# Attention scores of a Trainium2 megakernel: from masked f32 matmuls on 32 rows to bf16 parts on 72 rows, spread through DRAM

## The chip, the cores and the metric

One core of one Trainium2 chip runs the whole program. The metric is the device time of one execution in microseconds. The engines are PE (TensorE), DVE (VectorE), ACT (ScalarE), POOL (GpSimd) and SP (SyncE), which only issues transfers here.

## The reference, cut to what matters

The program chains four blocks over 8 sequences of 256 tokens and 128 features. The change is in the first of them, six layers of this:

```python
q = (h @ wq.T + bq_).reshape(bh, sl, H, DH)          # H = 16 heads of DH = 8
k = (h @ wk.T + bk_).reshape(bh, sl, H, DH)
scores = jnp.einsum('blhd,bmhd->bhlm', q, k) * inv_sqrt_d
w_avg = jax.nn.softmax(scores, axis=-1).mean(axis=1)
new_w = jax.nn.softmax(CSCALE * w_avg + rel[None], axis=-1)
sa = jnp.einsum('blm,bme->ble', new_w, h)
h1 = _ln(h + sa, l1w, l1b)
h2 = _ln(h1, l2w, l2b)
ff = jax.nn.relu(h2 @ w1.T + b1_) @ w2.T + b2_
return (_ln(h2 + ff, l3w, l3b), None)
```

Each head has only 8 dimensions, so a score is a sum of 8 products in f32.

## The kernel before

`stage_a` is the six layers; `stage_b`, `stage_c` and `stage_d` follow, each in a block of its own that starts when the one before has ended, and nothing in them changes. Stage A lasts from the start to about 1264 us.

The order of stage A is written out as a table of slots, `slots_a`. A sequence has 8 slots (`QSLOTS`); a slot covers 4 heads (`CH`) for one half of the 256 queries. Sequence `q` of layer `l` starts at slot `at = 64 * l + 8 * q`, and its later steps (mixing, normalizing, the hidden layer) stand at fixed slots behind that, so they fall beside the scores of the next sequences. In what follows "slot 0" to "slot 7" are slots modulo 8. Every engine walks the same table in order and skips what is not its own, so each engine's queue is strictly in table order; semaphores hold the engines together. Within a slot, `in_order` puts some kinds first and some last.

The steps of one slot: PE makes the scores of 4 heads into one of two PSUM buffers (`score`); DVE takes the negated row maximum of each half (`max0`, `max1`, L506); ACT makes the four exponentials one slot later (`exp`, L405); DVE inverts the row sums (L547) and adds two of the four heads into a PSUM sum (L483, L486, L495); POOL scales an identity matrix by the other two heads' inverse sums (`diag`, L308), with which PE adds those heads (`head_sum`, L639, last in its slot). `score` of a slot waits until the exponentials of two slots before have been read.

Steps once in a sequence that matter here, with their slots: DVE adds the hidden layer's output (L573) and takes its statistics (L521 with `a_h`) in slot 7; POOL turns them into a deviation (`rstd` part 2, L316 to L326), then applies the second gain (`affine` part 1, L352 and L355), both slot 7; DVE takes the statistics of the attended rows (L521 with `a_r`) in slot 0 and POOL turns these into a deviation (`rstd` part 0, again L316 to L326), slot 0; DVE normalizes with it (`norm` part 0, L528 with `a_r`), slot 1; POOL applies the first gain (`affine` part 0, L339 and L342, which reads `rows1`), slot 2; DVE takes the statistics of that in slot 4; `rstd` part 1 follows on POOL in slot 4. PE's last matmuls of the hidden layer (`mlp`, L673) stand in slot 7.

The scores before: `project` (slot 2) makes `qT` and `kT` in f32, `mask` on POOL (slot 3, last in the slot) writes `km`, four copies of `kT` each masked to one head of a 32-row group, and `score` runs two f32 matmuls of 32 rows and 512 columns side by side on two row groups.

SP loads the next layer's weights in a loop of its own, each group as soon as the last user of the old weights is done.

## Time and profile before

| | |
|---|---|
| median of 3 runs | 2278.96 us (2277.47 to 2282.62) |
| profiled execution, its own time | 2278.32 us |
| its span in the trace | 2276.4 us |
| busy share of the span: PE, DVE, ACT, POOL | 87%, 75%, 72%, 56% |
| granted clock of TensorE, mean | 0.955 |
| moved by DMA | 45.93 MB, mean 20 GB/s |

The shares are means over four stages, and PE's ends are modelled, so a PE that shows as busy need not be the limit. The profiled execution took 1.9 us more than its span, and 0.6 us less than the median.

### The profile page before, as it was taken

What the parts mean: (1) busy time and instruction counts of PE and PEld (TensorE: products, weight loads), DVE (VectorE), ACT (ScalarE), POOL (GpSimd) and SP (SyncE); (2) the same over time, 40 slices, a digit from 0 to 9 for tenths busy, and PEclk for the clock granted to TensorE, in tenths of its full rate; (3) what the DMA queues carried; (4) which work ended last, traced back from release to release, by engine and by line L of the source; (5) the groups of instructions that cost most, each with busy time, mean ns of one, the idle gap of its engine ahead of it and who ended that gap; (6) DMA issues with size and microseconds to landing.
All of it is one profiled execution on the core that took longest, in us unless ns stands there. A gap on an engine that the chain in (4) does not pass through costs nothing. (4 is left out here: it accounts for less than half of the span.)

```text
span 2276.4 us, 40732 instructions
## 1 busy us (share of the span) xinstructions
PE 1981.4 (87%) x9638; PEld 1254.6 (55%) x9638; DVE 1714.8 (75%) x4069; ACT 1647.2 (72%) x5239; POOL 1263.4 (56%) x2137
## 2 busy tenths in 40 slices
PE   4899999999999999999997784949995888898886
PEld 2455555555555555555555463336652666666665
DVE  5999999899899989999995425068876666766673
ACT  3888888788888878888884231459962778787874
POOL 2566766676667667667666333048874434443440
PEclk9999999999999999999998797869996999999999
DMA  1000000000000000000000311102212000000000
GB/s 44 1 1 4 7 13 4 3 17 4 5 7 13 4 3 17 4 4 7 13 1 1 130 53 48 30 19 93 101 56 72 1 1 1 1 1 1 1 1 19
DMA packets 30509, 45.93 MB, mean 20 GB/s; under 512 B 9352, under 2 KB 21904, under 8 KB 29952
## 3 DMA queue, kind: packets, MB, share of 16 engines
q1 hardware_dynamic: 29008, 40.52, 5.6%
q0 software_dynamic: 1248, 2.59, 0.3%
q8 instruction: 91, 1.49, 0.3%
q14 instruction: 162, 1.33, 0.2%
HBM read 39.34 MB, written 5.32 MB: 20 GB/s over the span
## 5 line engine op out<-in xcount | busy, mean ns | idle before, releaser
L405 ACT ACTIVATE a_prob<-a_scores,a_negmax 128x256 f32<-128x256 f32 x1536 | 706.2, 479 | 122.0 <-DVE a_negmax L506 91.7
L506 DVE TENSOR_REDUCE a_negmax<-a_scores 128x2 f32<-128x512 f32 x768 | 525.5, 685 | 53.3 <-PE a_scores L628 44.8
L628 PE MATMUL a_scores<-a_km,a_qT 32*128 32x512 f32 x1536 | 436.3, 646 | 63.2 <-ACT a_prob L405 56.2
L639 PE MATMUL a_heads<-a_prob,a_diag 128*128 128x256 f32 x1536 | 391.3, 388 | 11.0 <-POOL a_diag L308 7.5
L308 POOL TENSOR_TENSOR a_diag<-ident,a_rowinv 128x256 f32<-128x256 f32 x384 | 240.9, 632 | 157.4 <-DVE a_rowinv L547 150.3
L405 ACT ACTIVATION_READ_ACCUMULATOR a_prob<-a_scores,a_negmax 128x1 f32 x1536 | 323.2, 210 | 0.0
L639 PEld LDWEIGHTS a_heads<-a_prob,a_diag 128*128 128x128 f32 x1536 | 280.5, 193 | 62.8 <-POOL a_diag L308 25.1
L628 PEld LDWEIGHTS a_scores<-a_km,a_qT 32*128 32x128 f32 x1536 | 117.3, 184 | 196.2 <-issue 98.3
L1374 DVE TENSOR_TENSOR_SCAN c_state<-c_decay,c_psD 128x1024 f32<-128x1024 f32 x64 | 146.1, 2286 | 34.2 <-PE c_psD L1477 23.3
L1238 POOL TENSOR_TENSOR c_du<-c_state,c_c_row 128x1024 f32<-128x1024 f32 x64 | 151.3, 2366 | 33.6 <-DVE c_state L1374 24.3
L486 DVE SCALAR_TENSOR_TENSOR a_sums<-a_prob,a_rowinv,a_sums 128x256 f32<-128x256 f32 x288 | 141.1, 490 | 29.0 <-DVE a_rowinv L547 2.0
L316 POOL TENSOR_TENSOR a_f<-a_st 128x4 f32<-128x4 f32 x144 | 29.3, 203 | 201.2 <-DVE a_st L521 201.2
L495 DVE SCALAR_TENSOR_TENSOR a_sums<-a_prob,a_rowinv,a_sums 128x256 f32<-128x256 f32 x288 | 137.8, 478 | 0.0
L1818 ACT ACTIVATE d_prob<-d_psS,d_bias,d_inv 128x128 f32<-128x128 f32 (+1 forms) x256 | 121.7, 483 | 13.1 <-DVE d_bias L1952 12.3
L2041 PE MATMUL d_psQ<-d_wqkv,d_hT 128*128 128x512 f32 x192 | 105.6, 635 | 21.6 <-DVEq L1999 19.0
L1768 POOL TENSOR_TENSOR d_qk<-d_direct,d_cross 128x512 f32<-128x512 f32 x32 | 40.6, 1268 | 150.0 <-DVE d_cross L1925 150.0
L2082 PE MATMUL d_psO<-d_val,d_probT 128*128 128x64 f32 x768 | 101.1, 268 | 21.9 <-DVE d_o_n L1964 21.9
L1496 PE MATMUL c_psY<-c_du,ident 128*128 128x512 f32 x256 | 120.1, 593 | 0.0
L666 PE MATMUL a_turn<-a_h2T,a_w 128*128 128x256 f32 x384 | 110.6, 413 | 1.4 <-DVEq L564 0.7
L673 PEld LDWEIGHTS a_turn<-a_w,a_act 128*128 128x128 f32 x768 | 92.4, 197 | 35.1 <-issue 34.1
L2082 PEld LDWEIGHTS d_psO<-d_val,d_probT 128*128 128x128 f32 x768 | 95.8, 192 | 25.6 <-issue 25.6
L666 PEld LDWEIGHTS a_turn<-a_h2T,a_w 128*128 128x128 f32 x384 | 67.5, 194 | 76.4 <-issue 69.3
(286 smaller groups left out, 4282.8 us busy)
## 6 DMA issues: line engine op xcount, KB each, us to landing
c_c_row<-c_rows SPq DMA_DIRECT2D x32, 512.0 KB, 3.6
a_w<-in_a_w SPq DMA_DIRECT2D x12, 256.0 KB, 2.6
b_w<-in_b_w SPq DMA_DIRECT2D x1, 2816.0 KB, 15.2
a_rows<-in_a_rows SPq DMA_DIRECT2D x12, 128.0 KB, 2.0
b_w<-in_b_w SPq DMA_DIRECT2D x1, 1536.0 KB, 18.2
d_wqkv<-in_d_wqkv SPq DMA_DIRECT2D x2, 768.0 KB, 5.7
b_rows_in<-in_b_blank SPq DMA_DIRECT2D x1, 1518.0 KB, 8.8
b_packed<-b_rows_in SPq DMA_DIRECT2D x5, 264.0 KB, 4.2
```

The lines of the kernel that those rows point to most:

```text
L308: g.tensor_tensor(diag[part % RING][:], ident[:].unsqueeze(1).broadcast_to([P, BH, P]), rowinv[part % RING][:, 1::BH].unsqueeze(2).broadca ...
L405: ins = a.activation(prob[part % RING][:, c, :], psS[part % 2][:, c, :], ACT.Exp, bias=negmax[part % 2][:, c:c + 1], accum_out=rowsum[part ...
L486: v.scalar_tensor_tensor(psA[:, t, :], pr[:, 0, :], inv[:, 0:1], psA[:, t, :], ALU.mult, ALU.add).then_inc(s["acc_step"], 1)
L495: v.scalar_tensor_tensor(dst[:, t, :], prob[part % RING][:, BH, :], rowinv[part % RING][:, BH:BH + 1], psA[:, t, :], ALU.mult, ALU.add).th ...
L506: v.tensor_reduce(negmax[part % 2][:, hs], psS[part % 2][:, hs, :], AX.X, ALU.max, negate=True).then_inc(s["negmax_ready"], 1)
L628: p.matmul(psS[part % 2][:, h * BH:(h + 1) * BH, :], qT[u][rows, t * P:(t + 1) * P], km[u][rows, c:c + BH, :], start=True, stop=True)\
L639: ins = p.matmul(psH[:, t, :], diag[part % RING][:, h, :], prob[part % RING][:, h * BH + 1, :], start=(j == 0 and h == 0), stop=(j == HG - ...
L666: ins = p.matmul(dst[:, k, :], w1[:, f * P:(f + 1) * P], h2T[u][:], start=True, stop=True)
L1238: g.tensor_tensor(yc[n % 2][t], state[n % 2][t][:], c_row[n % CROWS][:], ALU.mult)\
L1374: v.tensor_tensor_scan(state[n % 2][t][:], decay[n % 2][t][:].rearrange("p q l -> p (q l)"), psD[t][:], 0.0, ALU.mult, ALU.add).then_inc(s ...
L1818: ins = a.activation(prob[t][g % 2][:, j, k0:k1], psS[n % 2][:, j, k0:k1], ACT.Exp, bias=bias[n % 2][:, j:j + 1], scale=inv[q % 2][t][:, 0 ...
L2082: ins = p.matmul(psO[:, h * DHD:(h + 1) * DHD], probT[g % 2][:, j, b, :], val[q % 2][:, b, h * DHD:(h + 1) * DHD], start=(b == 0), stop=(b ...
```

## The change

q and k are each written as a sum of three bf16 numbers (24 bits of mantissa in all). ACT rounds both to bf16 (one more ACTIVATE of 128x512 in `project`), and POOL makes the two remainders in three operations of 128x512 (`split`, in place of `mask`). SP writes the three parts to a DRAM scratch and reads them back in another layout (`spread`): 72 rows hold, for each of the 8 dimensions, the 9 pairs of a part of q with a part of k. For that the keys' 24 rows are read three times over, and each of q's three parts is read three times over. The weights' rows are sorted by dimension on the host. A head's scores are then one bf16 matmul with 72 rows and 256 columns, four to a slot, and the first half's semaphore rises after two of them.

The projection, the split and the spread of a sequence stand 10, 9 and 8 slots ahead of its first score; `project` was 6 ahead and `mask` 5. Because SP now takes part in the table, its loads of the next layer's weights stand in it too (`load`, parts 0 to 4), at slots -7, 25, 30, 34 and 40 of the last sequence of a layer.

```diff
-RG = 4
-RW = P // RG
+PARTS = 3
+KROWS = PARTS * PARTS * DH
+SPREAD = 16 + PARTS * 16 + 16
...
-                place(at - 8, "per_layer", l, q, 0)
-            place(at - 6, "project", l, q, 0)
-            place(at - 5, "mask", l, q, 0)
+                place(at - 12, "per_layer", l, q, 0)
+            place(at - 10, "project", l, q, 0)
+            place(at - 9, "split", l, q, 0)
+            place(at - 8, "spread", l, q, 0)
...
+            if q == SEQS - 1 and l + 1 < LAYERS:
+                for part, slot in enumerate((-7, 25, 30, 34, 40)):
+                    place(at + slot, "load", l, q, part)
...
-        qT = two("qT", [P, L])
-        kT = sb("kT", [P, L])
-
-        km = two("km", [P, CH, L])
-        head_mask = sb("head_mask", [P, CH])
+        qk = sb("qk", [P, 2, L])
+        rest = sb("rest", [P, 2, L])
+        one = sb("one", [P, 2])
+        parts3 = ctx.enter_context(nc.sbuf_tensor("a_parts3", [P, 2, PARTS, L], BF16))
+
+        spread = [[ctx.enter_context(nc.sbuf_tensor(f"a_spread{u}_{k}", [KROWS, HEADS, L], BF16)) for k in range(2)]
+                  for u in range(2)]
+        scratch = nc.dram_tensor("a_split", (2, PARTS, P, L), BF16, kind="Internal").ap()
+        keys = scratch[1].rearrange("a (e h) t -> (a e) (h t)", h=HEADS).unsqueeze(0)\
+            .broadcast_to([PARTS, PARTS * DH, HEADS * L])
+
+        def queries(a):
+            return scratch[0, a].rearrange("(e h) t -> e (h t)", h=HEADS).unsqueeze(0)\
+                .broadcast_to([PARTS, DH, HEADS * L])
...
-                    sp.wait_ge(s["qk_ready"], n * 2)
-                    load(l + 1, *qk)
-                    sp.wait_ge(s["n1_ready"], n)
-                    sp.wait_ge(s["h2_ready"], n)
-                    load(l + 1, *norm1)
-                    sp.wait_ge(s["act_ready"], n * FC)
-                    load(l + 1, *hidden)
-                    sp.wait_ge(s["y_ready"], n)
-                    load(l + 1, *out)
-                    sp.wait_ge(s["hT_ready"], n + SEQS)
-                    sp.wait_ge(s["h_tok_ready"], n + SEQS)
-                    load(l + 1, *norm3)
+
+                def do(kind, lay, steady, q, part):
+                    m = lay * SEQS + q
+                    u = q % 2
+                    if kind == "spread":
+                        sp.wait_ge(s["split_step"], (m + 1) * 4)
+
+                        sp.wait_ge(s["spread_in"], m * SPREAD + SPREAD)
+                        sp.dma_start(scratch.rearrange("k a p t -> p (k a) t"),
+                                     parts3[:].rearrange("p k a t -> p (k a) t")).then_inc(s["spread_in"], 16)
+                        sp.wait_ge(s["spread_in"], m * SPREAD + 16 + SPREAD)
+
+                        sp.wait_ge(s["scores_ready"], ((m - 2) * G8 + G8 + 2 * G8) * HALVES)
+                        sp.dma_start(spread[u][1][:], keys).then_inc(s["spread_in"], 16)
+                        for a in range(PARTS):
+                            sp.dma_start(spread[u][0][a * PARTS * DH:(a + 1) * PARTS * DH], queries(a))\
+                                .then_inc(s["spread_in"], 16)
+                    elif kind == "load":
+                        n = (lay + 1) * SEQS
+                        if part == 0:
+                            sp.wait_ge(s["qk_ready"], n * 2)
+                        elif part == 1:
+                            sp.wait_ge(s["n1_ready"], n)
+                            sp.wait_ge(s["h2_ready"], n)
+                        elif part == 2:
+                            sp.wait_ge(s["act_ready"], n * FC)
+                        elif part == 3:
+                            sp.wait_ge(s["y_ready"], n)
+                        else:
+                            sp.wait_ge(s["hT_ready"], n + SEQS)
+                            sp.wait_ge(s["h_tok_ready"], n + SEQS)
+                        load(lay + 1, *groups[part])
...
-                    elif kind == "mask":
-                        g.wait_ge(s["qk_ready"], m * 2 + 2)
-
-                        g.wait_ge(s["scores_ready"], ((m - 2) * G8 + G8 + 2 * G8) * HALVES)
-                        g.tensor_tensor(km[u][:], kT[:].unsqueeze(1).broadcast_to([P, CH, L]),
-                                        head_mask[:].unsqueeze(2).broadcast_to([P, CH, L]), ALU.mult)\
-                            .then_inc(s["km_ready"], 1)
+                    elif kind == "split":
+                        g.wait_ge(s["split_step"], m * 4 + 1)
+                        g.tensor_tensor(rest[:], qk[:], parts3[:, :, 0], ALU.subtract).then_inc(s["split_step"], 1)
+                        g.wait_ge(s["split_step"], m * 4 + 2)
+                        g.tensor_tensor(parts3[:, :, 1], rest[:], one[:].unsqueeze(2).broadcast_to([P, 2, L]), ALU.mult).then_inc(s["split_step"], 1)
+                        g.wait_ge(s["split_step"], m * 4 + 3)
+                        g.tensor_tensor(parts3[:, :, 2], rest[:], parts3[:, :, 1], ALU.subtract)\
+                            .then_inc(s["split_step"], 1)
...
-                run(g, do, first=("diag",), last=("mask",))
+                run(g, do, first=("diag",), last=("split",))
...
-                        a.wait_ge(s["scores_ready"], ((m - 2) * G8 + G8 + 2 * G8) * HALVES)
-                        a.activation(qT[u][:], src[:, 0, :], ACT.Identity, bias=bqs[:], scale=float(DH) ** -0.5)\
+                        a.wait_ge(s["split_step"], m * 4)
+                        a.activation(qk[:, 0, :], src[:, 0, :], ACT.Identity, bias=bqs[:], scale=float(DH) ** -0.5)\
                             .then_inc(s["qk_ready"], 1)
-
-                        a.wait_ge(s["km_ready"], m)
-                        a.activation(kT[:], src[:, 1, :], ACT.Identity, bias=qk_cols[:, 1:2])\
+                        a.activation(qk[:, 1, :], src[:, 1, :], ACT.Identity, bias=qk_cols[:, 1:2])\
                             .then_inc(s["qk_ready"], 1)
 
                         a.wait_ge(s["qk_ready"], 2 * m + 2)
                         a.sem_inc(t_free[b], 1)
+
+                        a.wait_ge(s["spread_in"], (m - 1) * SPREAD + 16 + SPREAD)
+                        a.activation(parts3[:, :, 0], qk[:], ACT.Copy).then_inc(s["split_step"], 1)
...
-                        evacuated("project")
-                        p.wait_ge(s["km_ready"], m + 1)
+                        if part == 0:
+                            p.wait_ge(s["spread_in"], (m + 1) * SPREAD + SPREAD)
 
                         p.wait_ge(s["exp_done"], (n + 1) * HALVES)
-                        for h in range(HALVES):
-                            rg = (j % 2) * HALVES + h
-                            rows = slice(rg * RW, (rg + 1) * RW)
-                            c = j // 2 * BH
-                            p.matmul(psS[part % 2][:, h * BH:(h + 1) * BH, :], qT[u][rows, t * P:(t + 1) * P],
-                                     km[u][rows, c:c + BH, :], start=True, stop=True)\
-                                .then_inc(s["scores_ready"], 1)
+                        for c in range(CH):
+                            ins = p.matmul(psS[part % 2][:, c, :], spread[u][0][:, j * CH + c, t * P:(t + 1) * P],
+                                           spread[u][1][:, j * CH + c, :], start=True, stop=True)
+                            if c % BH == BH - 1:
+                                ins.then_inc(s["scores_ready"], 1)
...
-    a["a_wq"] = np.ascontiguousarray(i["L0_attn_Wq"].transpose(0, 2, 1))
-    a["a_wk"] = np.ascontiguousarray(i["L0_attn_Wk"].transpose(0, 2, 1))
+    by_dim = lambda w: w.reshape(LAYERS, HEADS, DH, -1).transpose(0, 2, 1, 3).reshape(LAYERS, E, -1)
+    a["a_wq"] = np.ascontiguousarray(by_dim(i["L0_attn_Wq"]).transpose(0, 2, 1))
+    a["a_wk"] = np.ascontiguousarray(by_dim(i["L0_attn_Wk"]).transpose(0, 2, 1))
```

On POOL, this is the place from slot 7 to slot 2 in the last layer. `a_h` is the second normalization's result, `a_f` and `a_mv` are the statistics and the deviation, `a_diag` the scaled identity, `a_n` the first normalization's result. Before:

```order
L352 TENSOR_TENSOR a_h<-a_n,a_rows 128x256
L355 TENSOR_TENSOR a_h<-a_h,a_rows 128x256
L308 TENSOR_TENSOR a_diag<-ident,a_rowinv 128x256
L316 TENSOR_TENSOR a_f_1<-a_st_1 128x2x2
L317 TENSOR_TENSOR a_f_1<-a_st_1 128x2
L319 TENSOR_TENSOR a_f_1<-a_f_1,a_parts 128x6
L321 TENSOR_TENSOR a_mv_1<-a_f_1 128x2
L322 TENSOR_TENSOR a_mv_1<-a_f_1,a_eps 128x2
L324 TENSOR_TENSOR a_mv_1<-a_mv_1 128x2
L326 TENSOR_TENSOR a_mv_1<-a_mv_1,minus_half 128x2
L308 TENSOR_TENSOR a_diag<-ident,a_rowinv 128x256 x2
```

In the changed kernel (its line numbers are some 36 higher):

```order
L388 TENSOR_TENSOR a_h<-a_n,a_rows 128x256
L391 TENSOR_TENSOR a_h<-a_h,a_rows 128x256
L333 TENSOR_TENSOR a_rest<-a_qk,a_parts 128x512
L335 TENSOR_TENSOR a_parts<-a_rest,a_one 128x2x256
L337 TENSOR_TENSOR a_parts<-a_rest,a_parts 128x2x256
L344 TENSOR_TENSOR a_diag<-ident,a_rowinv 128x256
L352 TENSOR_TENSOR a_f_1<-a_st_1 128x2x2
L353 TENSOR_TENSOR a_f_1<-a_st_1 128x2
L355 TENSOR_TENSOR a_f_1<-a_f_1,a_parts 128x6
L357 TENSOR_TENSOR a_mv_1<-a_f_1 128x2
L358 TENSOR_TENSOR a_mv_1<-a_f_1,a_eps 128x2
L360 TENSOR_TENSOR a_mv_1<-a_mv_1 128x2
```

The three operations of `split` (`a_rest`, `a_parts`) now stand between the second gain and the next `a_diag`, ahead of the deviation that DVE's normalization in slot 1 reads. The masking stood in slot 3, behind the gains.

On SP, this is what the steady loop issues; `a_rows` are the gains of the normalizations, `a_w` the hidden layer's weights, `a_cols` and `a_b` small columns. Before, the whole loop body:

```order
L249 DMA a_wq<-in_a_wq 128x128
L249 DMA a_wk<-in_a_wk 128x128
L249 DMA a_qk_cols<-in_a_qk_cols 128x2
L249 DMA a_rows<-in_a_rows 128x256
L249 DMA a_rows<-in_a_rows 128x384
L249 DMA a_cols<-in_a_cols 128x2
L249 DMA a_w<-in_a_w 128x512
L249 DMA a_b<-in_a_b 128x4
L249 DMA a_w<-in_a_w 128x512
L249 DMA a_rows<-in_a_rows 128x256
L249 DMA a_cols<-in_a_cols 128x2
```

In the changed kernel, from the spread of a new layer's fourth sequence on (`a_split` is the DRAM scratch, `a_spread_1` the keys, `a_spread_0` the queries):

```order
L281 DMA a_split<-a_parts 128x6x256
L286 DMA a_spread_1<-a_split 72x1x4096
L288 DMA a_spread_0<-a_split 24x1x4096 x3
L263 DMA a_rows<-in_a_rows 128x256
L263 DMA a_rows<-in_a_rows 128x384
L263 DMA a_cols<-in_a_cols 128x2
L263 DMA a_w<-in_a_w 128x512
L263 DMA a_b<-in_a_b 128x4
L281 DMA a_split<-a_parts 128x6x256
L286 DMA a_spread_1<-a_split 72x1x4096
L288 DMA a_spread_0<-a_split 24x1x4096 x3
L263 DMA a_w<-in_a_w 128x512
```

Each load now stands behind the spreads of the sequences ahead of it in the table: the first gains (`a_rows`, 128x256) behind that of the fourth sequence of the new layer, the output weights (the second `a_w`) behind that of the fifth.

## Rows read from the trace of the kernel before

**Rows 1.** Windows: stretch, busy us of each engine (instructions), clock, DMA share, GB/s.

```profile
100.00:1230.00 1130.00, 1067.91 (x4896) 627.40 (x4897) 1015.11 (x2539) 935.33 (x3572) 765.88 (x1741) 0.99 0.02 7
```

**Rows 2.** Instruction groups, DVE, 100 to 1260 us: busy, mean ns, idle before and releaser.

```profile
L506 DVE TENSOR_REDUCE a_negmax<-a_scores 128x2 f32<-128x512 f32 x721 | 493.6, 685 | 36.1 <-PE a_scores L628 36.0
```

**Rows 3.** Timeline of DVE, one sequence: start us, us, instruction, idle before it.

```profile
569.49 0.41 DVE L573 TENSOR_TENSOR a_h<-a_h,a_turn 128x256 f32<-128x256 f32 x1
570.06 0.49 DVE L521 BATCH_NORM_STATS2 a_st<-a_h 128x6 f32<-128x128 f32 x2 [0.15 <-DVE a_h L573]
...
571.15 0.68 DVE L506 TENSOR_REDUCE a_negmax<-a_scores 128x2 f32<-128x512 f32 x1
...
576.88 0.89 DVE L528 TENSOR_SCALAR a_r<-a_r,a_f,a_mv 128x128 f32<-128x128 f32 x2
...
586.62 0.69 DVE L506 TENSOR_REDUCE a_negmax<-a_scores 128x2 f32<-128x512 f32 x1 [0.23 <-PE a_scores L628]
...
594.57 0.49 DVE L521 BATCH_NORM_STATS2 a_st<-a_h 128x6 f32<-128x128 f32 x2 [0.15 <-DVE a_h L573]
```

**Rows 4.** Timeline of POOL over the same sequence.

```profile
570.62 0.20 POOL L316 TENSOR_TENSOR a_f<-a_st 128x4 f32<-128x4 f32 x1 [3.31 <-DVE a_st L521]
...
573.49 0.72 POOL L355 TENSOR_TENSOR a_h<-a_h,a_rows 128x256 f32<-128x256 f32 x1
574.17 0.62 POOL L308 TENSOR_TENSOR a_diag<-ident,a_rowinv 128x256 f32<-128x256 f32 x1
574.74 0.20 POOL L316 TENSOR_TENSOR a_f<-a_st 128x4 f32<-128x4 f32 x1
...
576.14 0.71 POOL L326 TENSOR_TENSOR a_mv<-a_mv,minus_half 128x2 f32<-128x2 f32 x1
...
578.51 0.91 POOL L339 TENSOR_TENSOR a_n<-a_r,a_rows 128x256 f32<-128x256 f32 x1
579.49 0.73 POOL L342 TENSOR_TENSOR a_n<-a_n,a_rows 128x256 f32<-128x256 f32 x1
...
588.28 1.36 POOL L308 TENSOR_TENSOR a_diag<-ident,a_rowinv 128x256 f32<-128x256 f32 x2
```

**Rows 5.** Timeline of PE, same stretch.

```profile
566.32 1.13 PE L628 MATMUL a_scores<-a_km,a_qT 32*128 32x512 f32 x4
567.38 2.05 PE L673 MATMUL a_turn<-a_w,a_act 128*128 128x128 f32 x16
...
571.44 1.89 PE L639 MATMUL a_heads<-a_prob,a_diag 128*128 128x256 f32 x8
```

**Rows 6.** Instruction groups of POOL, whole run, shapes apart.

```profile
L300 POOL TENSOR_TENSOR a_km<-a_kT,a_head_mask 128x1024 f32<-128x1024 f32 x48 | 90.8, 1892 | 5.7 <-ACT a_kT L392 5.7
...
L1768 POOL TENSOR_TENSOR d_qk<-d_direct,d_cross 128x512 f32<-128x512 f32 x32 | 40.6, 1268 | 150.0 <-DVE d_cross L1925 150.0
...
L1777 POOL TENSOR_TENSOR d_qk<-d_direct,d_inv 128x512 f32<-128x512 f32 x32 | 33.4, 1042 | 5.7 <-POOL d_inv L1773 5.5 <-PE d_psT L2071 0.2
```

**Rows 7.** DMA issues by line: count, KB each, median us from issue to landing.

```profile
c_c_row<-c_rows SPq DMA_DIRECT2D x32, 512.0 KB, 3.6
...
out<-x_tok SPq DMA_DIRECT2D x1, 1024.0 KB, 5.1
...
a_wq<-in_a_wq SPq DMA_DIRECT2D x6, 64.0 KB, 1.9
```

**Rows 8.** Windows, a stretch full of transfers of stage B, columns as in Rows 1.

```profile
1283.00:1288.00 5.00, 5.00 (x12) 2.93 (x13) 2.22 (x6) 1.50 (x2) 2.47 (x3) 0.51 0.98 420
```

**Rows 9.** Page, part 3: the DMA queue of SP: packets, MB, share of 16 engines.

```profile
q1 hardware_dynamic: 29008, 40.52, 5.6%
```

**Rows 10.** Timeline, start of stage A, POOL and DVE.

```profile
29.19 1.89 POOL L300 TENSOR_TENSOR a_km<-a_kT,a_head_mask 128x1024 f32<-128x1024 f32 x1 [5.24 <-ACT a_kT L392]
...
33.32 2.48 DVE L506 TENSOR_REDUCE a_negmax<-a_scores 128x2 f32<-128x512 f32 x4 [8.37 <-issue]
```

**Rows 11.** Waits of POOL, 100 to 1230 us: us in total, times, longest.

```profile
POOL a_n L339 <- DMA a_rows<-in_a_rows: 1.0, 3, 0.4
```

More of the change, by code:

```diff
@@ L249, in load @@
                         sp.dma_start(dst[:], d[name][l]).then_inc(s[signal], 16)
-                qk = ("qk_in", (wq, "a_wq"), (wk, "a_wk"), (qk_cols, "a_qk_cols"))
-                norm1 = ("norm1_in", (rows1, "a_rows1"), (rows2, "a_rows2"))
-                hidden = ("hidden_in", (cols2, "a_cols2"), (w1, "a_w1"), (b1, "a_b1"))
-                out = ("out_in", (w2, "a_w2"))
-                norm3 = ("norm3_in", (rows3, "a_rows3"), (cols3, "a_cols3"))
-                for group in (qk, norm1, hidden, out, norm3):
-                    load(0, *group)
@@ L274, in _ @@
+                run(sp, do)
             @block.gpsimd
@@ L278, in _ @@
                 g.memset(eps[:], EPS)
+                g.memset(one[:], 1.0)
                 g.memset(minus_one[:], -1.0)
```

19 lines of the change are left out of this document (11 added, 8 removed).

## The prediction

> **What bounds the kernel now.** I read the windows first. Between 100 and 1230 us, in stage A's steady part, DVE is busy 1015 of 1130 us (90%), ACT 83%, POOL 68%; PE shows 94%, but its ends are modelled, so I ask who waits for whom [rows 1]. The groups of instructions say it for DVE: of its idle time only 36 us stood before a row maximum and ended with PE's scores [rows 2]; nearly all the rest is the gap behind its own last result. So DVE sets the pace, and PE's scores can give back at most about 36 us, 0.8 per sequence.
>
> The timelines show how near other engines are to setting it. One sequence takes 24.5 us, from DVE's statistics in slot 7 at 570.06 to the same at 594.57; I call that start T [rows 3]. At T + 0.56 POOL, idle 3.31 us for it, begins the deviation, then the second gain, at T + 4.1 the scaled identity, at T + 4.7 the next deviation, whose last operation ends at 576.85, T + 6.8 [rows 4]. DVE's normalization that reads it starts at 576.88 [rows 3]. There is no slack on this stretch: POOL works through it without a gap, and DVE arrives as it ends. POOL's 3.31 us of idle time lie ahead of it and can't be used by work queued behind. The masking, 1.89 us, stands in slot 3, where nobody waits for POOL.
>
> **The split on POOL.** The masking goes (nothing gained, no wait behind it). In its place come three operations of 128x512 between the second gain and the identity, in the middle of that stretch. With two full f32 operands POOL takes 1.27 us for this shape, with one operand repeated along a row 1.04 [rows 6]; the first and third are of the one kind, the second of the other. That is 3.58, and with a step of some 0.07 us between dependent operations, as from 579.42 to 579.49 [rows 4], 3.7 us. No row has bf16 on POOL. Bounds: three times half of the masking, 2.8, and three times 1.27 with gaps, 4.0; I take 3.7, since the shape and operands are those of the rows. DVE's normalization then comes 3.7 us late in each sequence. Queued behind POOL's split are the identity of slot 0, for which PE's head sum of slot 1 and so PE's score of slot 2 wait, but DVE stands still longer than they do. Sequences 3 to 47 have a split with such a deviation behind it: 45 x 3.7 = **+166 us**, and a sequence of 24.5 + 3.7 - 0.8 = 27.4 us, the last term being the next paragraph's.
>
> **The scores on PE.** Two f32 halves now run side by side and take 1.13 us for the four records [rows 5]; both are ready near the end. Four bf16 matmuls of 256 columns stream a quarter of the f32 columns each, and the first half is ready after two. No row has such a matmul with 72 rows; the change lies between nothing (1.13 as now) and about 0.9 us earlier for the first half. DVE's waits are short, 0.23 us in such a row [rows 3], so I take all of them away: **-36 us**, and nothing more, since PE is off the path.
>
> **ACT.** One more activation of 128x512, some 0.6 us, and the projection moved from slot 2 to slot 6. ACT's exponentials of slots 7 and 0 come some 1.6 us later, but they feed DVE between T and its normalization, where it has 3.7 us to spare. Cost nothing; without that cover up to 0.6 us for each of 48.
>
> **The spread, per sequence.** SP writes 0.39 MB in pieces of 512 bytes; the output copy has 1024 KB of such pieces and lands in 5.1 us, of which 1.75 is fixed by the 64 KB row (1.9 less its own data), so 1.75 + 0.375 x 3.35 = 3.0, with issue 3.1 [rows 7]. Then it reads 72 rows of 8 KB twice, 1.18 MB. The price hangs on how many DMA engines carry this. In a full stretch an engine moves 420 / (0.98 x 16) = 26.8 GB/s [rows 8]; over the whole run SP's queue gives 40.52 MB / (0.056 x 16 x 2276 us) = 19.9 GB/s [rows 9]. On 16 engines at the first rate the data take 2.75 us; on 3 they take 14.7, at the second rate 19.8. The trace has no landing of a copy with an outermost count below 16. The repeated row of 512 KB lands in 3.6 us [rows 7], so it has all engines, but its repeat is 128, outermost. Here the source is 3 x 24 (or 3 x 8) rows, the 3 outermost, against 72 (or 24) on the other side. I take sharing out along the outermost count that both sides have, so **3 engines**: from the end of the split to the first score 0.1 + 3.1 + 0.1 + 1.75 + 14.7 = 19.8 us. It has 7 slots and more.
>
> The Trainium skill (DMA: Bandwidth & Descriptors, "Why a DMA increments its semaphore by 16 and not by 1") says that a copy runs on the largest number of engines up to 16 that divides both outermost counts; by that it is 3 for these four copies and 16 for the write. No run here shows it yet.
>
> Does that bind in the steady part? Split end is at T + 7.8, its score is wanted one sequence later, at T + 27.4 + 0.6: 20.2 us on. So 19.8 just fits; above it DVE's spare time to the normalization covers another 4 us. Cost nothing.
>
> **The loads of the next layer**, queued behind the spreads on SP and on the same engines. Before, they came just in time: POOL waited 0.4 us at most for the first gains [rows 11]. Now three groups land behind 19.8 us of spread, at about T + 28, in each of 5 layer changes.
> - Part 0 (projection weights), wanted by PE's projection of slot 6 before T + 22, arrives at T + 27.9. Then projection 1.2, head sum 1.0, score, and the hidden layer's last matmuls, 2.05 [rows 5], so DVE's statistics come at T + 34.0 instead of 27.4: 6.6 us.
> - Part 1 (first gains), wanted by POOL in slot 2 at 578.51 [rows 4], T + 8.5 and now T + 12.1, arrives at T + 28.4. Behind it on POOL are its two gains, 1.7, then the identity of slot 3, 0.6; for that PE's two head sums wait, 1.9 [rows 5], then a score and its latency, 0.7: DVE's maximum of slot 5 at T + 33.3. It stood at 586.62 [rows 3], T + 16.6, and would now be at 19.9: 13.4 us.
> - Part 3 (output weights) is wanted by PE at 567.38 [rows 5], 2.7 before a T, so at T + 24.7, and arrives at T + 28.2: 3.5 us.
> Parts 2 and 4 have slots to spare. 5 x 23.5 = **+117 us**.
>
> **The start.** The masking began at 29.19 and the first maximum followed at 33.32 [rows 10]. The activation adds 0.7, the split 3.7 - 1.9, the spread 19.8: **+22 us**.
>
> **Sum** against the profiled execution's own time (0.6 below the median, nothing at this size): 2278.3 + 166 - 36 + 117 + 22 = 2547.3, rounded up for a PE whose clock may fall in the long pauses: **2548 us**.
>
> **Rivals.**
> - *All 16 engines carry the reads* (0.25). For it: every copy in the rows. Then the spread takes about 8 us with its four issues, parts 0 and 3 arrive in time, part 1 at T + 16.6, which leads to 21.5 against 19.9, 1.6 us five times; start 10.5. 2278.3 + 166 - 36 + 8 + 10.5 = 2427. By the rule of the Trainium skill cited above this would not happen.
> - *Three engines at the slower rate* (0.1): 24.9 us of spread. Each arrival is 5.1 later, 15 x 5.1 = 77; two sequences then take 24.9 + 31 us (from a first maximum at 571.15 to the statistics at 594.57, less the 0.8 gained, 22.7; from there to the split's end 7.8; 0.5 from landing to maximum), so 27.95 each for 27.4, 45 x 0.55 = +25; start +5. 2547 + 107 = 2654.
> - *PE was the limit, and POOL's idle time takes the split* (0.04; the other side). If PE's ends tell the truth, a faster PE lets DVE reach the statistics of slot 7 up to 3.3 us earlier against the rest, POOL's idle time [rows 4] goes into the stretch, and the split costs 0.4 per sequence net: with 16 engines 2278.3 - 36 + 18 + 10.5 = 2271. It decides when less than 0.6 us of the split is left on the stretch (25.5 / 45). Against it: DVE waits 0.8 us per sequence for PE, not 3.3 [rows 2].
> - *A dearer split or slower scores* (0.1): POOL at 5 us for the three would add 58, scores as late as now 36.
>
> **How the numbers follow.** The forecast's case has 0.5; its own range is 2500 to 2600 (split 2.8 to 4.0: -40 to +14; waits not gained +36). The other cases reach down to 2427 and up to 2654; with some of the split's bounds the range is 2410 to 2670, which leaves out 0.15. A measurement can tell about 0.2% from no change. Faster by more: 0.04; within: 0.01; slower: 0.95.
>
> **What would show it.** POOL: three operations of 128x512, 1.27, 1.04, 1.27 us, and behind them DVE's normalization (`a_r`) waiting some 3.6 us for `a_mv` in each sequence; DVE's waits for `a_scores` near zero in the steady part. The reads of the scratch land 16 us or more after issue (3 engines) or about 5 (16). POOL's first gain waits for `a_rows` by some 16 us five times, PE for the projection and output weights. A sequence takes 27.4 us. I am wrong if the copies use all engines, if bf16 costs POOL otherwise, or if PE or ACT falls behind DVE once everything is shifted by a stretch.

## The result, and the profile after

The changed kernel takes 2615.4 us (median of 4 runs, 2613.2 to 2620.3), the kernel before on the same chip 2278.2: a ratio of 1.148 with a 95% interval of 1.146 to 1.150. That is 337 us slower where 269 were forecast, and 67 us above the forecast of 2548. The windows show all engines of stage A less busy than before [rows 1]; the columns are those of rows 1.

```profile
100.00:1230.00 1130.00, 764.06 (x3794) 587.40 (x3794) 829.43 (x1980) 748.80 (x2819) 646.00 (x1413) 0.83 0.16 55
```

DVE fell from 90% to 73% (829 of 1130 us) and no other engine took its place: time went into waits in a ring. DVE's waits, 100 to 1500 us (total, times, longest), then POOL's and PE's for transfers:

```profile
DVE a_r L565 <- POOL a_mv L362: 99.2, 42, 2.6
DVE a_negmax L543 <- PE a_scores L662: 67.2, 25, 9.4
DVE a_st L558 <- POOL a_n L378: 65.9, 5, 14.1
DVE a_h L610 <- PE a_turn L708: 49.0, 29, 7.1
DVE a_rowinv L584 <- ACT a_prob L442: 28.8, 49, 3.0
```

```profile
POOL a_n L375 <- DMA a_rows<-in_a_rows: 91.7, 5, 19.3
POOL a_bqs L330 <- DMA a_qk_cols<-in_a_qk_cols: 39.4, 5, 8.3
...
PE a_turn L651 <- DMA a_qk_cols<-in_a_qk_cols: 28.5, 4, 7.5
PE a_turn L708 <- DMA a_w<-in_a_w: 24.8, 5, 5.4
PE a_scores L662 <- DMA a_spread<-a_split: 8.0, 5, 1.8
```

The first row comes about once in a sequence: that is the split. Those that wait four or five times, for long, for weights or gains are the layer changes. PE's five short waits for the spread are not: they fall in ordinary sequences too, the one at 692.43 among them. DVE's timeline over one sequence, the place of [rows 3], shows the first. T is, as in the prediction, the start of DVE's statistics `a_st<-a_h` in slot 7; the stretch runs from T to the normalization of `a_r`:

```profile
663.13 0.49 DVE L558 BATCH_NORM_STATS2 a_st<-a_h 128x6 f32<-128x128 f32 x2 [0.15 <-DVE a_h L610]
...
669.45 1.43 DVE L565 TENSOR_SCALAR a_n<-a_h,a_f,a_mv 128x128 f32<-128x128 f32 x2
673.47 0.89 DVE L565 TENSOR_SCALAR a_r<-a_r,a_f,a_mv 128x128 f32<-128x128 f32 x2 [2.60 <-POOL a_mv L362]
...
684.94 0.18 DVE L584 RECIPROCAL a_rowinv<-a_rowsum 128x4 f32<-128x4 f32 x1 [0.38 <-ACT a_prob L442]
...
687.64 0.18 DVE L584 RECIPROCAL a_rowinv<-a_rowsum 128x4 f32<-128x4 f32 x1 [0.26 <-ACT a_prob L442]
...
691.00 0.42 DVE L610 TENSOR_TENSOR a_h<-a_h,a_turn 128x256 f32<-128x256 f32 x1 [0.65 <-PE a_turn L708]
691.57 0.49 DVE L558 BATCH_NORM_STATS2 a_st<-a_h 128x6 f32<-128x128 f32 x2 [0.15 <-DVE a_h L610]
```

POOL over the same stretch, for [rows 4]:

```profile
666.58 0.72 POOL L391 TENSOR_TENSOR a_h<-a_h,a_rows 128x256 f32<-128x256 f32 x1
667.26 1.16 POOL L333 TENSOR_TENSOR a_rest<-a_qk,a_parts 128x512 f32<-128x512 f32 x1
668.49 1.04 POOL L335 TENSOR_TENSOR a_parts<-a_rest,a_one 128x512 bf16<-128x512 f32 x1
669.61 1.18 POOL L337 TENSOR_TENSOR a_parts<-a_rest,a_parts 128x512 bf16<-128x512 f32 x1
670.76 0.61 POOL L344 TENSOR_TENSOR a_diag<-ident,a_rowinv 128x256 f32<-128x256 f32 x1
```

From T to the normalization DVE now takes 10.34 us (663.13 to 673.47), before 6.82; the sequence takes 28.44 (to 691.57), before 24.5. So 3.5 us lie in the stretch, and the rest of the sequence, 18.10 us, is 0.4 longer than before, though 0.8 shorter was forecast. Only part of POOL's time shows as a wait: DVE's normalization just ahead (`a_n`) took 1.43 us beside POOL's split where 0.59 is its length in a kernel with the split elsewhere or its operations cut short, and ends inside what would be waiting anyway.

The starts of DVE's statistics in the timelines give the length of every sequence. These are eight in a row around one layer change, the same eight for each kernel (the others repeat the pattern). The named columns are the sequences that hold a load of the next layer: part 0, then 1, then 3. The last column is the median of each kernel's runs.

| kernel | part 0 | | | | part 1 | part 3 | | | sum | run, us |
|---|---|---|---|---|---|---|---|---|---|---|
| before | 24.5 | 24.7 | 27.9 | 24.5 | 24.5 | 25.0 | 24.5 | 24.5 | 200.1 | 2278.2 |
| changed | 36.8 | 28.6 | 30.5 | 28.4 | 42.4 | 34.2 | 28.4 | 29.0 | 258.3 | 2615.4 |
| wide reads | 28.1 | 29.6 | 31.2 | 28.4 | 34.9 | 29.0 | 28.9 | 28.7 | 238.8 | 2492.3 |
| loads first | 29.6 | 28.2 | 30.7 | 29.7 | 28.6 | 28.7 | 28.4 | 28.1 | 232.0 | 2477.2 |
| split in slot 3 | 24.1 | 24.1 | 29.8 | 24.3 | 33.5 | 24.5 | 23.9 | 23.9 | 208.1 | 2334.3 |
| all three | 24.1 | 24.1 | 31.0 | 24.3 | 24.2 | 25.9 | 24.0 | 23.9 | 201.5 | 2278.3 |

### The profile page after: what moved, and what is told of

It is laid out like the page before. It is cut to its first block and busy times, and to the rows that moved or that the text cites. A ratio compares the mean times of both kernels' runs of the same rounds, so it can differ in the third digit from the quotient of the medians.

```text
span 2611.4 us, 40935 instructions
## 1 busy us (share of the span) xinstructions
PE 1878.3 (72%) x9638; PEld 1384.8 (53%) x9638; DVE 1761.7 (67%) x4069; ACT 1675.7 (64%) x5287; POOL 1336.5 (51%) x2234
## 5 line engine op out<-in xcount | busy, mean ns | idle before, releaser
L674 PE MATMUL a_heads<-a_prob,a_diag 128*128 128x256 f32 x1536 | 491.7, 462 | 265.0 <-POOL a_diag L344 261.3
L674 PEld LDWEIGHTS a_heads<-a_prob,a_diag 128*128 128x128 f32 x1536 | 330.8, 230 | 349.0 <-POOL a_diag L344 286.1
L662 PE MATMUL a_scores<-a_spread,a_spread 72*128 72x256 bf16 x1536 | 281.5, 315 | 173.8 <-ACT a_prob L442 128.1
L662 PEld LDWEIGHTS a_scores<-a_spread,a_spread 72*128 72x128 bf16 x1536 | 160.6, 112 | 299.6 <-ACT a_prob L442 169.4
L442 ACT ACTIVATION_READ_ACCUMULATOR a_prob<-a_scores,a_negmax 128x1 f32 x1536 | 316.8, 206 | 0.0
L708 PE MATMUL a_turn<-a_w,a_act 128*128 128x128 f32 x768 | 107.6, 299 | 39.2 <-DMA a_w<-in_a_w 24.8
L708 PEld LDWEIGHTS a_turn<-a_w,a_act 128*128 128x128 f32 x768 | 100.1, 211 | 47.8 <-DMA a_w<-in_a_w 21.2
L2076 PE MATMUL d_psQ<-d_wqkv,d_hT 128*128 128x512 f32 x192 | 105.6, 635 | 21.6 <-DVEq L2034 19.0
L701 PE MATMUL a_turn<-a_h2T,a_w 128*128 128x256 f32 x384 | 117.2, 436 | 1.5 <-DVEq L601 0.8
L565 DVE TENSOR_SCALAR a_r<-a_r,a_f,a_mv 128x128 f32<-128x128 f32 x96 | 41.4, 471 | 105.6 <-POOL a_mv L362 105.6
```

Of the source, the lines that this page charges most:

```text
L442: ins = a.activation(prob[part % RING][:, c, :], psS[part % 2][:, c, :], ACT.Exp, bias=negmax[part % 2][:, c:c + 1], accum_out=rowsum[part ...
L662: ins = p.matmul(psS[part % 2][:, c, :], spread[u][0][:, j * CH + c, t * P:(t + 1) * P], spread[u][1][:, j * CH + c, :], start=True, stop= ...
L674: ins = p.matmul(psH[:, t, :], diag[part % RING][:, h, :], prob[part % RING][:, h * BH + 1, :], start=(j == 0 and h == 0), stop=(j == HG - ...
L708: ins = p.matmul(dst[:, 0, t * E:(t + 1) * E], act[:, f, t * P:(t + 1) * P], w2[:, f, :], start=(f == 0), stop=(f == FC - 1))
L2076: p.matmul(psQ[i % 2][:], hT[q % 2][:, t * P:(t + 1) * P], wqkv[q // SEQS][:, part, :], start=True, stop=True).then_inc(s["q_full"], 1)
```

## Experiments

Each kernel is the changed one with the edit shown; ratios are to the kernel before on the same chip, with 95% intervals. The kernels ran on several chips, where the kernel before took 2278 to 2283 us, so times of two kernels from different chips compare to about 5 us only.

**Wide reads.** The same bytes, with the 24 (or 8) rows outermost instead of the 3.

```diff
-.rearrange("a (e h) t -> (a e) (h t)", h=HEADS).unsqueeze(0)
-    .broadcast_to([PARTS, PARTS * DH, HEADS * L])
+.rearrange("a (e h) t -> (a e) (h t)", h=HEADS).unsqueeze(1)
+    .broadcast_to([PARTS * DH, PARTS, HEADS * L])
...
-return scratch[0, a].rearrange("(e h) t -> e (h t)", h=HEADS).unsqueeze(0)
-    .broadcast_to([PARTS, DH, HEADS * L])
+return scratch[0].rearrange("a (e h) t -> e a (h t)", h=HEADS)
```

> Only the four reads of a spread change: the same rows in another order (key part, dimension, query part), so that the outermost count of the source is 24 for the keys and 8 for the queries, not 3. Theory (three engines carried the reads, and the loads of the next layer queue behind them): the reads end some 10 us earlier, the DMA share rises and their time falls; the start gains about 10 us, the three stalls at each of 5 layer changes shrink from 28 to about 4 us, so 2615 - 10 - 124 = about 2480 us; the 10.3 us stretch from the statistics of slot 7 to DVE's normalization stays. Rival (the engines were not the limit, the memory or the queue was): no change, 2615.

Measured: 2492.3 us, 1.091 (1.089 to 1.094), 12 us above the expectation: the sequence of the first gains still takes 34.9 us. The first maximum comes 9.0 us earlier (46.44 for 55.44). In the changed kernel a window inside the reads shows a share of 0.20 at 82 GB/s, which is 3/16 = 0.19 of the engines and 82 / (0.20 x 16) = 26 GB/s for each:

```profile
677.00:689.00 12.00, 9.52 (x52) 6.93 (x50) 10.67 (x28) 11.08 (x42) 6.76 (x16) 0.98 0.20 82
```

With the wide reads two windows inside them show

```profile
594.00:595.00 1.00, 1.00 (x8) 0.91 (x8) 1.00 (x3) 0.84 (x2) 0.92 (x2) 1.00 0.81 156
595.00:596.00 1.00, 0.93 (x4) 0.50 (x4) 0.88 (x4) 0.80 (x3) 0.49 (x2) 1.00 0.78 246
```

A load of weights of 256 KB, issued at 592.62, is in these windows too. The reads' traffic lasts from 591 to about 599, 8 us, where it took some 14 in the changed kernel. So the order of the dimensions sets how many engines work. POOL's waits for `a_rows` fall from 91.7 to 47.0 us.

**Loads first.** Parts 0, 1 and 3 of the next layer's loads ahead of the spread they stood behind.

```diff
-                for part, slot in enumerate((-7, 25, 30, 34, 40)):
+                for part, slot in enumerate((-9, 24, 30, 32, 40)):
```

> Only the slots of three loads change (-7 to -9, 25 to 24, 34 to 32), so that SP issues the loads of parts 0, 1 and 3 ahead of the spread behind which they stood. Theory (the stalls at the layer changes are loads queued behind 15 us of spread on the same engines): the waits for a_rows, a_qk_cols and a_w fall to nothing, 2615 - 142 = about 2473 us, with the spread itself as slow as before and the start unchanged at 55.4 us to the first maximum. Rival (transfers of the spread slow everything at the layer change, or SP now holds up the spread): at least half of the 142 us stays.

Measured: 2477.2 us, 1.084 (1.081 to 1.087). The table shows all three peaks gone and the other sequences unchanged at 28 to 31 us. The layer changes cost 2615.4 - 2477.2 = 138 us; 117 were forecast. A cure for either the engines or the queue's order takes most of it.

**Split in slot 3.** Where the masking stood, with the projection in slot 2, as before.

```diff
-                place(at - 12, "per_layer", l, q, 0)
-            place(at - 10, "project", l, q, 0)
-            place(at - 9, "split", l, q, 0)
+                place(at - 16, "per_layer", l, q, 0)
+            place(at - 14, "project", l, q, 0)
+            place(at - 13, "split", l, q, 0)
...
-                for part, slot in enumerate((-7, 25, 30, 34, 40)):
+                for part, slot in enumerate((-13, 25, 30, 34, 40)):
```

> Projection and split stand 14 and 13 slots ahead (slots 2 and 3, where projection and masking stood), per_layer 16, the load of part 0 at -13; the spread stays at -8. Theory (POOL's split lies on the stretch between DVE's statistics of slot 7 and its normalization of slot 1, and ACT's crowded slot 6 costs about 1 us more per sequence): DVE's waits for a_mv (99 us) and for ACT vanish, 2615 - 158 - 50 = about 2405 us, 6.8 us again for the stretch. Rival (POOL's added work is the cost wherever it stands): 2500 or more, with POOL's waits moved to slots 3 to 5.

Measured: 2334.3 us, 1.022 (1.019 to 1.024), 71 less than expected. The stretch is back at 6.83 us (median of all sequences) and a sequence takes 23.9, less than the 24.5 of before. The expectation left the layer changes at their full price, but projection and loads of part 0 are early now and its peak is gone, that of part 3 is gone too though its load kept its slot (24.5 for 34.2), and that of part 1 fell from 14.0 us above its neighbours to 9.6.

**Tiny split.** All waits and transfers kept, POOL's three operations cut to 2 columns.

```diff
-tensor_tensor(rest[:], qk[:], parts3[:, :, 0], ALU.subtract)
+tensor_tensor(rest[:, :, 0:2], qk[:, :, 0:2], parts3[:, :, 0, 0:2], ALU.subtract)
```

(and the same for the other two, with the buffer cleared at the start).

> The changed kernel with POOL's three split operations cut from 256 to 2 columns of each of q and k, all waits, the spread and the slots kept (two of the three parts are left zero but for these columns, so small errors are left in the scores). Theory (the three operations stand on the stretch from DVE's statistics to its normalization): that stretch falls from 10.3 to about 7.2 us and the sequence to about 25, 45 x 3.5 = 158 less: about 2455; the layer changes keep their waits. Rival (the spread's transfers or the POOL handovers cost it, not the operations): 2560 or more.

Measured: 2491.4 us, 1.092 (1.088 to 1.095): 124 less, where 158 were expected. The median stretch fell from 10.34 to 7.56 us, by 2.8 for 3.5 expected; the small operations still stand there. 45 x 2.8 = 125. So the length of the three operations is what DVE waits for; the layer changes kept their peaks (34.0, 40.5, 31.8). One of its sequences, from T to the normalization and to the next T:

```profile
643.01 0.49 DVE L559 BATCH_NORM_STATS2 a_st<-a_h 128x6 f32<-128x128 f32 x2 [0.15 <-DVE a_h L611]
...
649.61 0.59 DVE L566 TENSOR_SCALAR a_n<-a_h,a_f,a_mv 128x128 f32<-128x128 f32 x2
650.56 0.89 DVE L566 TENSOR_SCALAR a_r<-a_r,a_f,a_mv 128x128 f32<-128x128 f32 x2 [0.35 <-POOL a_mv L363]
...
668.41 0.49 DVE L559 BATCH_NORM_STATS2 a_st<-a_h 128x6 f32<-128x128 f32 x2 [0.15 <-DVE a_h L611]
```

This run shows one thing more. The part of a sequence behind the stretch, from the normalization to the next T, did not get shorter with the stretch: over the 29 of the first 44 sequences that hold none of the three loads, it is 0.59 us longer than before on average, here as in the changed kernel. So DVE's long wait for POOL is not by itself what makes that part longer. What it goes with is the granted clock. Before, the clock is full there and the part takes 17.5 to 17.9 us. In this kernel it is full in nine of the 29, and eight of these take 17.6 to 18.1 us (the ninth stands at the end of the stage). In the changed kernel it is full in none: where it is 0.88 to 0.92 on average the part mostly takes 17.6 to 18.4 us, and where it is 0.76 to 0.78, 19.3 to 19.4. A window within the part in this kernel's sequence (17.85 us), then two in the changed kernel's, of 18.10 and of 19.34 us (columns as in rows 1):

```profile
651.00:668.00 17.00, 12.79 (x74) 9.82 (x74) 15.26 (x37) 13.88 (x51) 9.03 (x20) 1.00 0.18 71
```

```profile
674.00:691.00 17.00, 14.48 (x76) 10.90 (x74) 14.81 (x37) 13.84 (x50) 8.98 (x20) 0.90 0.18 70
963.00:981.00 18.00, 15.91 (x74) 12.40 (x74) 14.85 (x36) 14.63 (x54) 8.80 (x19) 0.78 0.17 67
```

No run holds the clock fixed, so this is a pattern in the traces and not an experiment.

**Scores alone.** No split, no spread, no rounding on ACT: the bf16 matmuls run on operands that were cleared once, so the attention weights are not the reference's. `project` stays in slot 6.

```diff
-            place(at - 9, "split", l, q, 0)
-            place(at - 8, "spread", l, q, 0)
...
-                        a.activation(parts3[:, :, 0], qk[:], ACT.Copy).then_inc(s["split_step"], 1)
```

> Leaves out the split, the spread and ACT's rounding; the score matmuls read operands that are zero and were set once at the start, so the attention weights are not the reference's. What is left of the change are the bf16 matmuls and the projection in slot 6. Theory (the matmuls give back DVE's waits for scores and nothing else): 2278 - 36 = about 2242 us, up to 10 more for clearing the operands at the start. Rival A (the bf16 matmuls with four weight loads are no faster for DVE): 2278. Rival B (PE had been the limit): 2150 or less.

Measured: 2297.9 us, 1.006 (1.004 to 1.007), 56 above the expectation and 15 above the kernel before on that chip (2283.4). Little of it is the start: the first maximum comes at 42.51 instead of 33.32, behind the clearing, but the first T at 127.68 instead of 124.47, 3.2 us later. The other 11 us lie in the sequences, most of which take 24.5 to 25.3 us for 24.3 to 24.7. The matmuls themselves got shorter: four records take 0.60 us for 1.13, and DVE's waits for scores, 36 us before, are 8.2. But other waits took their place:

```profile
DVE a_h L607 <- PE a_turn L705: 38.4, 39, 7.9
DVE a_rowinv L581 <- ACT a_prob L439: 22.4, 43, 3.1
...
DVE a_negmax L540 <- PE a_scores L659: 8.2, 10, 1.3
```

```profile
PE a_turn L705 <- ACT a_mixT L460: 26.5, 39, 0.8
```

PE's last matmuls of the hidden layer wait for ACT, which now has the projection in slot 6 beside its own work there (the second normalization on `a_n`, and `a_mixT`). Of the 38.4 us of the first row, 13.5 fall behind 1250 us, in the last sequences, and the kernel below has such waits there too (16.3). That suggested the next kernel.

**Scores alone, projection in slot 2.** The same with `per_layer`, `project` and the load of part 0 as in the split-in-slot-3 kernel.

> As the kernel without split and spread (the bf16 scores on cleared operands, so the attention weights are not the reference's), with the projection in slot 2 instead of slot 6. Theory (ACT's crowded slot 6 ate what the shorter matmuls gave): the sequence falls from 24.72 to 23.9 us or less, 47 x 0.8 = 38 less: 2298 - 38 = about 2260, and DVE's waits for the exponentials fall. Rival (the shorter matmuls are simply worth nothing): 2298, sequence 24.7.

Measured: 2262.1 us, 0.991 (0.988 to 0.994), as the theory had it: 36 us less than the kernel above (34 by the two ratios), and the sequence falls from 24.7 to 24.0. DVE's waits on `a_h` and `a_rowinv` are down:

```profile
DVE a_h L607 <- PE a_turn L705: 16.3, 4, 8.1
...
DVE a_rowinv L581 <- ACT a_prob L439: 7.4, 22, 0.8
```

Both kernels have the short matmuls, so these 36 us are the price of the projection in slot 6, not the worth of the matmuls. The latter is read against the kernel before on the same chip, 2280.8: this kernel takes 18.7 us less, though its first T comes 5.3 later (129.75). So in place the matmuls gave back some 24 of the forecast 36 us, and moving the projection to slot 6 cost some 35, more than all of it.

**Projection in slot 2, split left in slot 7.** The full changed kernel with only that part of the edit.

> The changed kernel with only the projection moved from slot 6 to slot 2 (and what must stand ahead of it: the load of part 0 and the scaled bias); the split stays in slot 7. Theory (ACT's slot 6 is overfull, which costs the 1.1 us by which a sequence is longer than the forecast 27.4): 47 x 1.1 = 52 less, and the late projection weights, 5 x 6.6 = 33, vanish: 2615 - 85 = about 2530; the sequence takes 27.4 us. Rival (the 1.1 us come from something else, such as the DVE normalization slowed beside POOL's work): only the weights, about 2582, and the sequence stays at 28.5.

Measured: 2589.5 us, 1.135 (1.132 to 1.139); the rival's 2582, not the theory's 2530. Part 0's peak is gone (29.8 for 36.8), but the other sequences are not shorter, 28.6 to 30.9; behind the stretch the 29 without a load are 1.1 us longer than before, for 0.6 in the changed kernel. DVE's waits for ACT's exponentials doubled, from 28.8 to 58.1 us. The timelines of ACT suggest why. In the changed kernel, behind DVE's stall:

```profile
676.06 0.48 ACT L442 ACTIVATE a_prob<-a_scores,a_negmax 128x256 f32<-128x256 f32 x1 [5.47 <-DVE a_negmax L543]
...
688.26 0.60 ACT L463 ACTIVATE a_mixT<-a_turn 128x512 f32<-128x512 f32 x1
688.73 0.49 ACT L424 ACTIVATE a_qk<-a_turn,a_bqs 128x256 f32<-128x256 f32 x1
689.09 0.50 ACT L426 ACTIVATE a_qk<-a_turn,a_qk_cols 128x256 f32<-128x256 f32 x1
689.77 0.63 ACT L433 ACTIVATE a_parts<-a_qk 128x512 bf16<-128x512 f32 x1 [0.18 <-ACT a_qk L426]
```

When DVE stands still, ACT gets no new maxima and stands still 5.47 us too. Then it works from 676.06 to beyond 690 with pauses of at most 0.32 us. The projection and the rounding come last in that run, behind `a_mixT`, the last of ACT's results that DVE needs before the next T, so in slot 6 they are covered here. In slot 2 they stand at the head of the run:

```profile
666.36 0.47 ACT L424 ACTIVATE a_qk<-a_turn,a_bqs 128x256 f32<-128x256 f32 x1 [5.58 <-PE a_turn L651]
```

**Three tests of ACT.** In the changed kernel the rounding cut to 2 columns (its buffer cleared at the start), and the rounding done twice:

```diff
-a.activation(parts3[:, :, 0], qk[:], ACT.Copy)
+a.activation(parts3[:, :, 0, 0:2], qk[:, :, 0:2], ACT.Copy)
```

```diff
+a.activation(twice[:], qk[:], ACT.Copy)
 a.activation(parts3[:, :, 0], qk[:], ACT.Copy)
```

> The changed kernel with ACT's rounding cut from 256 to 2 columns of each of q and k (the first part is left zero but for these columns, so the scores lose accuracy and the second part takes its place); 0.63 us of ACT become about 0.2. Theory (in DVE's stall ACT has no new maxima and stands idle 5.5 us, then works without a pause until the next stall, so each us of ACT lies on the path): about 45 x 0.4 = 18 less, 2597. Rival (ACT's work is covered, as the forecast had it, and the 1.1 us are DVE's and PE's own): 2615, within 0.2%.

> The changed kernel with ACT's rounding of 128x512 done twice, the first time into a buffer that nobody reads: 0.53 to 0.63 us more of ACT in each sequence, in slot 6. Theory (ACT lies on the path behind DVE's stall): 45 x 0.55 = 25 more, 2640. Rival (covered): 2615.

Measured: 2604.4 us, 1.143 (1.140 to 1.145), and 2607.3 us, 1.143 (1.141 to 1.145). The cut operation takes 0.21 us and the two others 0.63 and 0.61; between the two kernels lies 1.03 us of ACT in each sequence and 3 us in all, where the theory had 43. Both ran on one chip, so this comparison carries more than the 8 to 11 us by which both lie below the changed kernel's time on another. The theory fell: the rounding in slot 6 costs nothing, as the prediction said. Then with the projection in slot 2 and two more roundings behind it:

> The kernel with only the projection moved to slot 2 (2589.5 us), with ACT's rounding of 128x512 done two more times into a buffer that nobody reads: 1.1 to 1.2 us more of ACT in each sequence, now just behind DVE's stall instead of in slot 6. Theory (DVE's stall idles ACT by 5.5 us too, ACT then works without a pause until slot 6, and only ACT's work in that run lies on the path; the rounding doubled in slot 6 cost nothing since DVE waits for nothing behind it before its next stall): 45 x 1.1 = 50 more, about 2640. Rival (it is PE's clock, half for some 6.5 us behind the stall, that makes the rest of the sequence long, and ACT never binds): 2590.

Measured: 2607.9 us, 1.143 (1.139 to 1.146), for 1.135 without them: about 18 us more, of 50 (by the two intervals 16, give or take 11). DVE's waits for ACT rise from 58.1 to 72.2 us, and the rest of a sequence behind the stretch from 19.1 to 20.0 us (medians; the two profiled executions lie 28 us apart, more than the medians of the runs). ACT's work at the head of its run does bind, but for about a third of it; neither expectation was right.

**All three cures.** Split in slot 3, wide reads, loads at (-13, 24, 30, 32, 40); and the same with the reads as in the changed kernel.

> The whole change with projection and split 4 slots earlier, one read row per dimension outermost (more engines), and the loads of part 0, 1 and 3 ahead of the spread they stood behind. With projection and split 4 slots earlier alone the sequence is 23.94 us against 24.5 before. Theory (what is left beside the start are the layer changes, because SP's loads land behind spreads): sequences -27 us, start +13, layer changes near 0: 2283 - 27 + 13 = about 2270, and POOL's waits for a_rows are gone. Rival (what is left is something of the changed kernel itself, such as PE's clock or ACT): only the start gets shorter, 2334 - 9 = about 2325.

> The kernel with projection and split 4 slots earlier and the loads ahead of the spreads, but with the reads as in the changed kernel (three outermost rows, so three engines). Theory (the engines of the reads matter only at the start once no load waits behind them and the spread stands 4 slots ahead of its use): 8 us more than with the wide reads, about 2287. Rival (the spread of three engines still binds in the steady part): 2300 or more.

Measured: 2278.3 us, 0.999 (0.997 to 1.000), the same as before within what can be measured; and 2309.2 us, 1.012 (1.010 to 1.015), 31 more where 8 were expected. With three engines the spread of one sequence in each layer change is late:

```profile
521.61 1.03 PE L662 MATMUL a_scores<-a_spread,a_spread 72*128 72x256 bf16 x4 [4.90 <-DMA a_spread<-a_split]
```

Five sequences of 28 to 30.5 us where the wide reads have 24.3 to 25.9 are that cost. Perhaps the loads put ahead of the spreads now push these back; that was not tried. In the kernel with all cures two costs are left. The first maximum comes at 46.75, 13.4 us later than before. And three times in the run, one of them in the table, a sequence takes 31 us for 27.9. There DVE stands for nothing that the profile shows, longer than before:

```profile
433.12 0.18 DVE L583 RECIPROCAL a_rowinv<-a_rowsum 128x4 f32<-128x4 f32 x1 [6.80 <-issue]
```

and in the kernel before:

```profile
422.50 0.18 DVE L547 RECIPROCAL a_rowinv<-a_rowsum 128x4 f32<-128x4 f32 x1 [2.97 <-issue]
```

That is 3 x 3.3 = 10 us more. The two costs, 23 us, are about what the other 44 sequences gain at some 0.4 to 0.6 us each. Why the second pause grew was not tried.

## Why the prediction was right in kind and 67 us short

The trace of the profiled executions gives the whole difference by place. A sequence runs from T to T; the stretch is its part up to the normalization, the rest what follows. The forecast's terms are put into the same places (its -36 us as 0.8 in the rest of each sequence):

| place | forecast | measured |
|---|---|---|
| up to the first T (124.47, then 147.33) | +22 | +22.9 |
| the stretches of the first 44 sequences | +166 | +148.4 |
| the rest of the 15 that hold a load of part 0, 1 or 3 | +117 - 12 | +150.2 |
| the rest of the other 29 | -24 | +17.1 |
| the last three sequences | 0 | -1.6 |
| sum, up to the last T (the span grew by 335.0) | +269 | +337.0 |

- **The split on POOL, +166: right.** The operations took 1.16, 1.04 and 1.18 us for 1.27, 1.04 and 1.27, and the stretch grew by 3.5 for 3.7. Cutting the operations and moving them both confirmed it.
- **The scores, -36, and the moved projection, nothing: the step that failed.** The prediction said of ACT "Cost nothing; without that cover up to 0.6 us for each of 48", and took the whole -36 for the scores. The table has +17 us where -24 stood for the 29 ordinary sequences, and some of the excess of the 15 others will be the same. Without the split the runs show how: the shorter matmuls are worth some 24 us if ACT keeps up, and the projection in slot 6 costs some 35 (2297.9 for 2262.1), because ACT's `a_mixT` is late for PE, and DVE waits for that and for the exponentials instead of for scores. I had priced the added activation and not the crowding of slot 6 by the moved projection. That is +11 for -36, 47 us, where the changed kernel is 67 above the forecast.
- **What stays open in it.** In the changed kernel itself the projection moved back to slot 2 gave nothing beyond the load of part 0, so the two costs do not simply add. The rounding is not the rest of it (cut or doubled, no effect in slot 6; two more in slot 2 cost a third of their time), nor is DVE's long wait or its slowed normalization (the tiny split has next to none of either and the same 0.59 us). PE's granted clock is the likeliest part: with the projection in slot 6 the part behind the stretch takes 17.6 to 18.1 us at full clock and up to 19.4 at 0.76. The prediction had rounded its sum up by 0.7 us for it. Its share was not isolated.
- **The spread on three engines: right.** The share of 0.20 and the wide reads show it. By the Trainium skill (DMA: Bandwidth & Descriptors, "Why a DMA increments its semaphore by 16 and not by 1") it is the largest count up to 16 that divides both outermost counts; the traces agree at 3. For the wide reads it would by that rule be 12 and 8, shares of 0.75 and 0.50; the measured ones, with other traffic among them, don't settle that. One sequence's spread took from the split's end at 670.79 to a score that had waited until 692.43, 21.6 us for 19.8: the four read issues on SP take 2.9 us, which I hadn't counted, though no run shows how much of the 1.8 is theirs. It nearly fits its slots, as said (PE waited 8.0 us in all).
- **The layer changes, +117: mechanism right, size small.** Above their neighbours' 28.4, the three peaks in the table are 8.4, 14.0 and 5.8 us for 6.6, 13.4 and 3.5; 28.2 for 23.5, five times 4.7 are 24 more. Measured by the loads put first: 138. The arrivals came at T + 29.6 to 31.3 for the forecast 27.9 to 28.4, some 2 us late each. After PE's idle 6.78 us in the layer change the granted clock was 0.50 from 750 to 755 (1.2 GHz for 2.4), and the projection took twice its 0.60 us.

```profile
750.51 1.22 PE L651 MATMUL a_turn<-a_hT,a_wq 128*128 128x256 f32 x2 [6.78 <-DMA a_qk_cols<-in_a_qk_cols]
...
754.83 0.69 DVE L543 TENSOR_REDUCE a_negmax<-a_scores 128x2 f32<-128x512 f32 x1 [8.69 <-PE a_scores L662]
```

- **The start, +22: right.** The first maximum moved from 33.32 [rows 10] to 55.44, 22.1 us:

```profile
55.44 2.49 DVE L543 TENSOR_REDUCE a_negmax<-a_scores 128x2 f32<-128x512 f32 x4 [30.00 <-issue]
```

- **The rivals.** All 16 engines: excluded by the share. Three engines at a slower rate: 26 GB/s per engine, so no. A dearer split: 3.38 us for the three, so no; slower scores: four records take 0.60 us for 1.13, so no. POOL's idle time taking the split: did not happen; POOL still idles ahead of the stretch as long as before (3.31 us, [rows 4]):

```profile
692.14 0.20 POOL L352 TENSOR_TENSOR a_f<-a_st 128x4 f32<-128x4 f32 x1 [3.63 <-DVE a_st L558]
```

The forecast's distance from the measured time is smaller than its errors: the stretches came out 18 us below it, the layer changes 45 above and the ordinary sequences 41 above.

## What to carry to other kernels

Work added to a side engine costs by where it stands in the ring of waits: the same three operations cost some 150 us ahead of a result that another engine awaits, and nothing that shows where the old masking had stood (a sequence of 23.9 us there, 24.0 in the kernel without them). A matmul made shorter gives back only what its other partners can deliver; price what moves with it, not only what is added. The price of a move holds for the kernel in which it was read: the projection's slot was worth 35 us without the split and nothing with it. When loads share a queue with new traffic, give each its place by the slot in which it is needed, and write a copy's pattern with the larger dimension outermost.
